# A second score product in place of transposed probabilities, and means in float32r parts, in a fused transformer kernel

## The reference, cut to what matters

```python
h = tok(x) ; h = concat([h, txt], axis=1)        # 128 samples, S = 97 tokens of 128
h = h + attnA(_layernorm(h))                     # A: retention with a decay mask
h = h + ffnB(_layernorm(h))                      # B and C
# A, for each of 8 heads of 16: q, k, v complex
scores = einsum('bhse,bhte->bhst', q, k) * decay ; y = einsum(scores, v).real
yn = (y - mean(y)) * rsqrt(var(y) + 1e-5) * gn_scale + gn_bias      # over the 16 of a head
out = (silu(x @ w1.real) * yn) @ w2.real
# B
q, k, v = x @ Wq + bq, x @ Wk + bk, x @ Wv + bv
attn = softmax(einsum('bqhd,bkhd->bhqk', q, k) / 4)
o = einsum('bhqk,bkhd->bqhd', attn, v) @ Wo + bo
h2 = _layernorm(x + o) * ln1_g + ln1_b
# C: the best of 8 experts by softmax(h2 @ gate_W + gate_b), gelu in its hidden layer of 512
out = gw * (gelu(h2 @ W1[e] + b1[e]) @ W2[e] + b2[e])
```

## Time and profile before

| | |
|---|---|
| median of 3 runs | 1347.37 us (1346.21 to 1348.26) |
| the profiled execution | 1349.02 us |
| its span, first to last instruction | 1347.2 us |
| TensorE, VectorE, ScalarE, GpSimd busy | 97%, 76%, 53%, 30% |
| granted clock of TensorE, mean | 0.993 |
| DMA | 124.60 MB, 92 GB/s |

### The profile page before, as it was taken

The page is one execution under the profiler, slowest core; times in us unless marked ns, Lnnn a source line. Parts: engine busy times, 40 slices in busy tenths (PEclk is TensorE's granted clock), DMA queues, the critical chain, the costliest instruction groups (busy, mean ns, idle before and its releaser), DMA issues.

```text
span 1347.2 us, 40101 instructions
## 1 busy us (share of the span) xinstructions
PE 1307.4 (97%) x14816; PEld 967.8 (72%) x14817; DVE 1024.1 (76%) x2332; ACT 715.1 (53%) x1632; POOL 409.0 (30%) x268
## 2 busy tenths in 40 slices
PE   7899999999999999999999999999999986999998
PEld 5566776666666666666676776666666655999998
DVE  2667777777777777777777877777877886777776
ACT  2345555555555555555555555555555555556565
POOL 0000222222222222222222222222222225666666
PEclk9999999999999999999999999999999998999999
DMA  9322323332333333332332322223332011443332
GB/s 389 132 75 75 88 88 88 88 88 88 88 88 88 88 88 88 88 88 86 87 86 79 85 86 86 86 88 88 88 88 64 15 30 39 119 126 103 103 103 65
DMA packets 95130, 124.60 MB, mean 92 GB/s; under 512 B 56619, under 2 KB 77149, under 8 KB 94592
## 3 DMA queue, kind: packets, MB, share of 16 engines
q1 hardware_dynamic: 38400, 102.47, 23.6%
q0 software_dynamic: 56576, 19.93, 6.9%
HBM read 101.27 MB, written 20.82 MB: 91 GB/s over the span
## 4 chain that ended last, share of the span: by engine, by line
PE 92%; DVE 3%; issue 2%; ACT 1%; DMA 1%; SPq 0%; DVEq 0%; POOL 0%; POOLq 0%; ACTq 0%
PE bank_emb L459 20%; PE bank_s L519 9%; PE bank_y L447 7%; PE bank_x L533 7%; PE bank_z L447 6%; PE bank_s L814 6%; PE bank_s L447 5%; PE bank_s L585 4%; PE bank_x L803 3%; PE bank_y L803 3%; PE bank_s L597 3%; PE bank_x L607 3%; PE bank_z L625 3%; PE bank_z L648 3%; PE bank_z L597 3%; PE bank_x L447 2%
## 5 line engine op out<-in xcount | busy, mean ns | idle before, releaser
L1703 POOL DMA_INDIRECT expert_rows<-row_sb,placei x128 | 275.5, 2152 | 321.0 <-issue 313.5
L459 PE MATMUL bank_emb<-home_x 128*128 128x256 f32 (+1 forms) x1216 | 335.2, 392 | 6.0 <-DMA home_x<-in_x_main 6.0
L459 PEld LDWEIGHTS bank_emb<-home_x 128*128 128x128 f32 (+1 forms) x1216 | 219.1, 192 | 123.6 <-issue 60.1
L1181 DVE TENSOR_TENSOR home_s<-bank_s,con 97x776 f32<-97x776 f32 x256 | 237.2, 957 | 15.9 <-PE bank_s L519 15.7
L1692 POOL COPY h<-txt 128x128 f32<-128x128 f32 x32 | 9.4, 294 | 545.7 <-DVE h L1231 521.9
L1720 POOL DMA_INDIRECT out_tokens<-yo,tok x104 | 123.9, 1192 | 69.5 <-issue 53.0
L519 PE MATMUL bank_s<-qm,xn 32*97 32x452 f32 x1024 | 131.7, 583 | 6.2 <-DVE home_s L1200 3.2
L1195 DVE TENSOR_REDUCE mx<-bank_s 97x8 f32<-97x776 f32 x128 | 117.9, 961 | 25.8 <-PE bank_s L585 25.7
L1200 DVE TENSOR_TENSOR home_s<-bank_s,mx 97x776 f32<-97x776 f32 x128 | 117.6, 958 | 0.1
L814 PE MATMUL bank_s<-w2e,home_s 128*128 x832 | 110.0, 275 | 0.0
L993 ACT COPY row_sb<-bank_z 97x272 f32<-97x272 f32 x58 | 22.5, 387 | 164.8 <-PE bank_z L648 164.5
(11 more groups left out here) (265 smaller groups left out, 2314.0 us busy)
## 6 DMA issues: line engine op xcount, KB each, us to landing
home_x<-in_x_main SPq DMA_DIRECT2D x96, 768.0 KB, 5.1
home_x<-expert_rows SPq DMA_DIRECT2D x104, 129.0 KB
w1e<-in_exp_w SPq DMA_DIRECT2D x1, 2576.0 KB, 11.7
txt<-in_txt_t SPq DMA_DIRECT2D x32, 64.0 KB, 8.9
w2e<-in_exp_w SPq DMA_DIRECT2D x1, 2048.0 KB, 17.1
expert_rows<-row_sb,placei POOLq DMA_INDIRECT x128, 8.7
out_tokens<-yo,tok POOLq DMA_INDIRECT x104, 2.5
home_x<-in_x_tail SPq DMA_DIRECT2D x32, 48.0 KB, 8.7
```

Of the source, the lines that this page charges most:

```text
L459: mm = pe.matmul(banks["emb"][:, 0:NPG], wtok[0:k, c, :], x_sb[0:k, c, :], start=(c == 0), stop=(c == KC - 1))
L1181: ins = dve.tensor_tensor(sm[:, k % 2, 2 * h:2 * h + 2, :], pair(h), decay, ALU.mult)
L1703: pool.indirect_dma_start(out=rows[:, :], out_offset=bass.IndirectOffsetOnAxis(ap=placei[:, k, c:c + 1], axis=0), in_=row_sb[:, k, c, E:E ...
```

## The change

*B's softmax.* The first score product stays, but only VectorE's maximum reads it; b_max now spreads the maxima over 128 columns (strip r, sample and head parity j at column 32r + 8j, the rest zero). TensorE transposes them (b_max_t), which puts each maximum on a spare partition of the strip, unused by the 16 features of the other head. VectorE adds them to the masked queries qx (b_query_max). The masked keys kx carry a -1 on that partition (kx_bias, from mark). The second score product (b_shifted) of kx and qx then yields score minus maximum, with keys on the partitions. ScalarE takes the exponential straight from PSUM into pt (b_exp). The eight sets of transposes, their copies and the shift are gone.

*Centering and means.* The five products with constant matrices are each split: ScalarE rounds the operand to float32r (the high part), VectorE subtracts it from the operand (the low part, float32r as well), and two float32r products add up in PSUM (halves). The constant matrices are exact in float32r.

*Keys and queries of B.* The masked keys go from VectorE to ScalarE (b_key), which also writes kx (b_key_marked, four operations of 194 columns) and qx (b_query_of).

*Order.* USES, all lists of a round and the lists of the last groups are new. All 19 embedding products of group i+1 stand in round i. A's first mix moves into its own group's round.

```diff
+            def halves(g, name, what, lhs, hi, lo):
+                pe.wait_ge(s_hi[what], g + 1)
+                ps = use(g, name)
+                pe.matmul(ps[:, 0:N], lhs, hi, start=True, stop=False)
+                pe.wait_ge(s_lo[what], g + 1)
+                done(pe.matmul(ps[:, 0:N], lhs, lo, start=False, stop=True), g, name)
...
             def a_var(g):
-                pe.wait_ge(s_sqa, g + 1)
-                product(g, "A.var", const("mean"), sqa[:])
+                halves(g, "A.var", "sqa", mean_r[:], a_hi[:], a_lo[:])
...
-            def b_probs_t(g, k, r):
-                name = f"B.probs_t{k}.{r}"
+            def b_max_t(g, k):
+                name = f"B.max_t{k}"
                 ps = use(g, name)
-                pe.wait_ge(s_prob, PROB[g, k, r // 2])
-                for j in range(4):
-                    t = slice(j * S, (j + 1) * S)
-                    mm = pe.transpose(ps[0:S, t], prob[:, k, r, t], const("ident")[0:S, 0:S])
-                done(mm, g, name)
+                for h in range(2):
+                    read(pe, g, f"B.scores{k}.{h}")
+                done(pe.transpose(ps[:, 0:S], mx[:, k, :], const("ident")[0:S, 0:S]), g, name)
+
+            def b_shifted(g, k):
+                for h in range(2):
+                    use(g, f"B.shifted{k}.{h}")
+                read(pe, g, f"B.max_t{k}")
+                for c in range(2):
+                    t = slice((2 * k + c) * S, (2 * k + c + 1) * S)
+                    for o in range(2):
+                        j = 2 * c + o
+                        for r in range(4):
+                            rows32 = slice(32 * r, 32 * r + 32)
+                            mm = pe.matmul(bank_s[0:S, r, j * S:(j + 1) * S], kx[rows32, o, t], qx[rows32, o, t],
+                                           start=True, stop=True)
+                            if j == 3 and r % 2:
+                                done(mm, g, f"B.shifted{k}.{r // 2}")
...
+            def high(g, what, dst, src):
+                act.copy(dst, src).then_inc(s_hi[what], 1)
...
+            def b_key_marked(g, o, last=False):
...
+                for c in range(2):
+                    j = 2 * (1 - o) + c
+                    ins = act.activation(kx[:, o, :].rearrange("p (k c t) -> p k c t", k=2, c=2)[:, :, c, :],
+                                         ps[:, 0:N].rearrange("p (k c t) -> p k c t", k=2, c=2)[:, :, c, :],
+                                         ACT.Identity, bias=kx_bias[:, j:j + 1], scale=const("odd" if o else "even"))
...
+                ins = act.activation(qx[:, o, :], ps[:, 0:N], ACT.Identity, bias=qx_col[:, 2 + o:3 + o],
+                                     scale=qx_col[:, o:o + 1])
...
-                p = prob[:, k, 2 * h:2 * h + 2, :].rearrange("p g t -> p (g t)")
-                act.activation(p, p, ACT.Exp).then_inc(s_prob, 1)
+                drain(act.activation(pt[:, k, 2 * h:2 * h + 2, :], pair(h), ACT.Exp), g, name)
...
+            def low(g, what, dst, src, hi):
+                dve.wait_ge(s_hi[what], g + 1)
+                dve.tensor_tensor(dst, src, hi, ALU.subtract).then_inc(s_lo[what], 1)
...
+            def b_query_max(g, k, o, last=False):
+                name = f"B.max_t{k}"
+                ps = full(dve, g, name)
+                q = qx[:, o, 2 * k * S:(2 * k + 2) * S].rearrange("p (c t) -> p c t", c=2)
+                ins = dve.scalar_tensor_tensor(out=q, in0=ps[:, 0:S].unsqueeze(1).to_broadcast([P, 2, S]),
+                                               scalar=const("even" if o else "odd"), in1=q, op0=ALU.mult, op1=ALU.add)
...
             for i in range(FIRST, STEADY):
-                at(text, i)
                 at(scatter, i - 4)
+                at(text, i + 1)
```

More of the change, by code:

```diff
@@ L18 @@
 F32 = mybir.dt.float32
+F32R = mybir.dt.float32r
 BF16 = mybir.dt.bfloat16
@@ L549, in b_center @@
             def b_center(g):
-                read(pe, g, "A.out")
-                product(g, "B.center", const("center"), h1[:])
+                halves(g, "B.center", "h1", center_r[:], b_hi[:], b_lo[:])
             def b_var(g):
-                pe.wait_ge(s_sqb, g + 1)
-                product(g, "B.var", const("mean"), sqb[:])
+                halves(g, "B.var", "sqb", mean_r[:], b_hi[:], b_lo[:])
             def b_q(g):
@@ L615, in b_mix @@
                     read(pe, g, "B.v")
-                for r in range(4):
-                    read(pe, g, f"B.probs_t{k}.{r}")
+                for h in range(2):
+                    read(pe, g, f"B.shifted{k}.{h}")
                 ps = use(g, "B.o") if k == 0 else banks[BANK_OF[g, "B.o"]]
@@ L1140, in _ @@
             dve.wait_ge(s_k, 32)
+            for o in range(2):
+                which = const("odd" if o else "even")
+                dve.tensor_scalar(qx_col[:, o:o + 1], which, 0.25, None, ALU.mult)
+                dve.tensor_scalar(qx_col[:, 2 + o:3 + o], column("bq"), which, 0.25, ALU.mult, ALU.mult)
+            dve.tensor_reduce(mark[:], const("ident").rearrange("p (r j z) -> p j r z", j=4, z=8)[:, :, :, 0], AX.X,
+                              ALU.add).then_inc(s_cols, 1)
+            dve.wait_ge(s_cols, 1)
+            for o in range(2):
+                m = slice(2 * (1 - o), 2 * (1 - o) + 2)
+                ins = dve.scalar_tensor_tensor(out=kx_bias[:, m], in0=const("odd" if o else "even").to_broadcast([P, 2]),
+                                               scalar=column("bk"), in1=mark[:, m], op0=ALU.mult, op1=ALU.subtract)
+            ins.then_inc(s_cols, 1)
             dve.tensor_copy(run[:], const("run0")).then_inc(s_zero, 1)
@@ L1166, in a_query_imag @@
                     drain(ins, g, "A.qi")
-            def b_key(g, half, last=False):
-                ps = full(dve, g, "B.k")
-                ins = dve.tensor_scalar(k2[:, half, :], ps[:, 0:N], const("odd" if half else "even"),
-                                        bko[:, half:half + 1], ALU.mult, ALU.add)
-                if last:
-                    drain(ins, g, "B.k")
             def a_decayed(g, k, h, last=False):
@@ L1528, in _ @@
+            y_gated(NG - 1)
+            b_residual(NG - 3)
+            b_query_max(NG - 2, 0, 1)
+            a_residual(NG - 1)
+            b_query_max(NG - 2, 0, 0, last=True)
+            b_query_max(NG - 2, 1, 0)
+            h1_low(NG - 1)
+            b_query_max(NG - 2, 1, 1, last=True)
+            exp_sum(NG - 4)
             place_all(NG - 4)
             run_on(NG - 4)
+            c_sum(NG - 3)
             place_chosen(NG - 4)
+            next(first, None)
             place_sum(NG - 4)
+            next(first, None)
@@ L1532, in _ @@
+            gate_weight(NG - 4)
+            next(first, None)
+            b_low(NG - 1)
+            next(first, None)
+            b_normal(NG - 1)
+            next(first, None)
+            c_scale(NG - 3)
+            next(first, None)
+            logits(NG - 3)
             next(first, None)
```

695 lines of the change are left out of this document (377 added, 318 removed), and 19 rows, old and new, of the table USES.

## The result

| | before | after |
|---|---|---|
| median | 1347.82 us (1346.21 to 1348.90, 4 runs) | 1287.0 us (1285.55 to 1289.57, 4 runs) |
| ratio | | 0.955 [0.9535, 0.9564] |
| profiled execution, its span | 1349.02, 1347.2 us | 1289.57, 1287.4 us |

What follows compares the result with a forecast made beforehand. TensorE's chain of steps was taken to bound each group: 1349.0 - 50.8 (29 groups x 1.75) - 3.8 (last groups) + 2 (start) = 1296.4, with the median 1.65 lower: 1295 us; 8-in-10 range 1276 to 1330.

Steps and rivals of the forecast that it cites:

- Transposes, second score product, float32r: TensorE per group: transposes removed -2.72 us, maxima transposes +0.22, second score product +1.29, five float32r pairs -1.62.
- The rivals on loads: Second score product: loads bind it at 40 ns, 1335 us, 0.08; loads one after another, 1426 or 1420, 0.02.
- that on the float32 rate: Five split products: float32r runs at the float32 rate, +4.9 us a group, 1447 us, chance 0.04.
- The group, -1.75 predicted: Sum of TensorE's terms in one steady group: -1.75 us, giving a group of 32.3 us.
- the switches: TensorE changes between full width, row strips and column strips: from 13 to 19 a group, mean 0.18 us each.
- the last of the rivals: Whole group: the old order's own stalls vanish, 0.7 us a group, 1274 us, chance 0.03.
- the order's term: TensorE's new order per group: six more tiling switches at a mean of 0.18 us, +1.08 us.
- VectorE and ScalarE: Work beside TensorE per group: VectorE stays at about 26 us, ScalarE goes from 18.4 to 21.2; both fit.
- The thin margins: Hand-overs between engines within a group: covered by 0.3 to 0.5 us at the tightest, nothing added to the forecast.
- The start: First centering waits for high and low parts and ScalarE's setup: +2 us, between 0 and +4.
- The last groups: Last steady round, without a next group's embedding products: about 28.5 us in place of 32.3, -3.8 us.
- The tail: From the last keys to the first expert tile's transpose: 0, between -5 and +5 us.

Runs made afterwards that it cites:

- both visits: Changed kernel with an embedding tile moved to add one row-strip visit a group: 1298.61 us; or one column-strip visit a group: 1336.06 us on the slower chip.
- The kernel with fillers: Changed kernel plus 27 unread products in TensorE's waits, last round and behind the last group: 1283.0 us, 0.9522; slower chip 1313.97 us, 0.9502.
- the column visit: Changed kernel with an embedding tile moved between two column-strip steps, one more visit a group: 1336.06 us, 0.9666, on the slower chip.
- the twins: Changed kernel with the second score product issued twice, added one with 48 moving columns: 1361.92 us; with 48 stationary columns too: 1352.64 us (slower chip).

## Why the prediction was right, and where its sizes were off

*What bounds it*: right. TensorE's chain set the group before and after, and its steps could be added up.

*Transposes, second score product, float32r*: right. The steps missed by little: pairs took 0.35 in place of 0.32, the transposed maxima 0.09 in place of 0.11. Added up by columns, a group was to lose 2.83 us and lost 2.86. The rivals on loads fell (the 64 loads of a group pass 20 ns apart, with no idle time of the products), that on the float32 rate too. The choice of one column a cycle was an argument from a bf16 row, and the record bore it out. Slips in the rivals' prices (1426 and 1420 count 32 groups, the others 31; 4 x 0.162 is a part's whole price at the float32 rate, of which 3 x 0.162 is the surplus) change nothing in the verdict.

*The group, -1.75 predicted and -2.18 measured* is the term that was mis-sized, 12 us of the total. Not the switches: both visits show 0.2 and 0.17 us a switch, and the 19 of the changed group, read off the chain, add up to some 3.7 us (as 0.94 for 0.75 of columns at 672.06). Six more cost 1.1 to 1.2. But all that lies above the columns grew only by 0.68 us, from 3.63 to 4.31, so 0.4 to 0.5 us a group of the old order's own losses went: the last of the rivals, which I had at 0.7 us and a chance of 0.03, came true by more than half. It comes out of three pieces of the old order. The first is in its densest stretch of small instructions, A's second mix behind B's sums and mix; the second is in a step that gives rows for routing (L648). From three windows of the chain before:

```profile
583.71 0.65 PE bank_z L648 x4
...
609.92 0.98 PE bank_x L533 x40
610.90 0.03 issue
610.92 0.70 PE bank_x L533 x17
...
848.49 1.35 PE bank_x L533 x60
```

The same mix takes 1.71 in one group and 1.35 in another. By the records of all 29 steady groups, 12 have this stretch 0.16 to 0.74 us longer than the shortest, 0.17 us a group in the mean; in the changed kernel's profiled execution every steady group takes 31.86 or 31.87 (when it ran again, two were 0.2 longer). The second step of rows (L648) takes 0.65 in every group, 0.19 more than its like at 684.74 after the change: its weight loads wait for ScalarE's copy (row_sb) out of the bank that both steps of rows use; in the changed order they use two banks. The eight transposes stood at 2.86 with their neighbours, not 2.72. Together this is 0.5 us a group. So the forecast's step that failed in size is the order's term: it counted the switches that come, +1.08, and put the old order's own waits at nothing. With switches of 1.1 to 1.2 and 0.5 of waits gone, the term measured +0.7.

*VectorE and ScalarE*: 26.1 and 20.9 us, near what was worked out, though single prices were off. On VectorE a low part takes 0.56 us (0.5 assumed). On ScalarE the keys and queries take 0.67 (0.59) and the halves of the marked keys 0.51 (0.4), while the exponentials got shorter from PSUM (0.81 after 0.84) where 0.06 more was assumed. That these cancel is luck. *The thin margins*: held; the one tested was 0.44 us where 0.5 was named.

*The start*: +2 predicted. The first centering is indeed 2.3 us later (23.51 against 21.18), by the wait for the high part, but at the third round's keys nothing is left of it, because the rounds up to there are already shorter. The prediction's sum holds one of them (29 x 1.75 where the table has 28 rounds). *The last groups*: -3.5 for -3.8. *The tail*: 0 was right within its bounds. The +4.1 of the profiled execution goes with TensorE's lower clock, which another execution of the same kernel shows for a shorter time, with a stretch of 55.3 us. With the clock held at 1.00 the stretch took 54.3 us; that the clock makes the whole difference is likely, not shown.

## What to carry over

Where the chain of waits is one engine's alone, a change can be priced from its steps: columns by rate, plus some 0.2 us here for each change of tiling, and the order's own losses, which a new order may remove or bring. Count in what the old chain shows above its columns, and ask of each piece whether the new order keeps it. A saving on the full engine is had only if the hand-overs that it adds find their place: a split that gave 1.5 us a group here cost some 8 in the old order. And a delay is read from start to start, not from the sum of records: three operations of 0.42 us delayed their neighbour by 0.91.

## What the runs showed of the hardware

*Two chips, one kernel, 2.4% apart.* The kernel with fillers took 1283.0 us on one and 1314.0 on the other, at the same granted clock of 1.00 in its steady part. Step by step the chains are alike, but for one stretch, where mixes and a score product follow each other in small instructions. On the faster chip:

```profile
419.69 1.35 PE bank_y L650 x64
421.03 0.67 PE bank_x L547 x32
421.71 0.86 PE bank_s L597 x16
```

On the slower:

```profile
427.01 1.49 PE bank_y L650 x62
...
428.58 0.68 PE bank_x L547 x30
...
429.62 0.99 PE bank_s L597 x14
```

2.88 against 3.61 us, +0.73 a group; the whole group is 0.78 longer. TensorE waits there for no engine. That its instructions arrive too slowly there fits this, the long second mix before, and the 0.24 us of "issue" in the column visit; no run changed the supply of instructions itself, so it remains a reading.

*float32r* of 388 columns takes 0.17 to 0.18 us, 1.1 cycles a column at 2.4 GHz, as one record; float32 takes 0.65, 4.0 cycles, as two.

*Four row strips* pass 16 float32 products (32 records, each with a load) of 32 rows with 97 moving and 97 stationary columns in 0.65 us, 20 ns for each load. The Trainium skill ("TensorE: Matmul & The Clock Gate", section "LDWEIGHTS (loading the stationary operand)") has a load take its columns over 1.2 GHz, an estimated 81 ns for 97. The trace agrees if four strips load at a time (81 / 4 = 20), and disagrees with loads one after another. By that rule alone half the columns would take half the time, where the twins went from 0.69 to 0.50.
